# The 64-row group of the layer-3 experts' second product as two 128x64 column tiles

## The reference, cut to what matters

```python
S, E, K, C = 1024, 8, 2, 320
probs = softmax(xr @ Wg)
gate_vals, expert_idx = top_k(probs, K)
# pos: place of each (token, choice) in its expert's queue; kept = pos < C
dispatched = xr[token_of_slot].reshape(E, C, 256)
h = relu(einsum('ecd,edf->ecf', dispatched, w1))     # w1: 8 x 256 x 1024
expert_out = einsum('ecf,efd->ecd', h, w2)           # w2: 8 x 1024 x 256
out = sum over k of combine_weight[k] * expert_out[slot of (token, k)]
x = x + tanh(g_ffn[3]) * out
```

## Time and profile before

| | |
|---|---|
| median of three runs | 944.33 us (943.89 to 945.1) |
| profiled execution, span from first to last instruction | 941.6 us (the page gives no other time for it) |
| mean granted TensorE clock over the span | 0.876 of full speed |
| TensorE matmul busy | 735.4 us, 78% of the span |
| VectorE busy | 551.5 us, 59% |
| ScalarE, GpSimd busy | 372.5 us, 343.9 us |
| layer-3 experts, from the first product to the end | about 762 to 941.6 us of the span |

### The profile page before, as it was taken

How to read it: one execution, slowest core, us unless ns; L and a number is a source line. 1 busy time by engine, 2 the same in 40 slices (tenths; PEclk the granted TensorE clock), 3 DMA queues, 4 the chain that set the end, 5 groups by cost and what they waited for, 6 DMA issues and landing times.

```text
span 941.6 us, 14328 instructions
## 1 busy us (share of the span) xinstructions
PE 735.4 (78%) x5159; PEld 509.5 (54%) x5204; DVE 551.5 (59%) x1280; ACT 372.5 (40%) x673; POOL 343.9 (37%) x364
## 2 busy tenths in 40 slices
PE   5987899992567777777797992693876489999998
PEld 3444554561535555555665881362444457777776
DVE  2897847329779999989368453928676520000004
ACT  4002033222389898989520333241663122111220
POOL 2931310654137776767303715500230170000124
PEclk9997899996779898988699996696988579999999
DMA  6311217895029999999811668100013144333413
GB/s 223 127 56 46 49 42 226 195 125 48 1 44 181 170 179 163 179 164 179 174 45 45 152 122 279 42 2 0 1 42 139 46 118 142 104 103 104 149 45 117
DMA packets 139218, 102.78 MB, mean 109 GB/s; under 512 B 109714, under 2 KB 124300, under 8 KB 137102
## 3 DMA queue, kind: packets, MB, share of 16 engines
q1 hardware_dynamic: 130472, 79.10, 34.8%
q0 software_dynamic: 7760, 22.16, 11.7%
q10 hardware_dynamic: 918, 0.62, 0.2%
HBM read 65.34 MB, written 11.33 MB: 81 GB/s over the span
## 4 chain that ended last, share of the span: by engine, by line
PE 33%; issue 13%; DVE 11%; ACT 4%; DMA 3%; POOL 3%; POOLq 0%; DVEq 0%; ACTq 0%
PE psum L2291 8%; PE psum L2273 7%; PE psum L1608 3%; DVE xnT L1399 2%; PE psum L214 2%; PE psum L1885 2%; ACT both L1292 2%; DMA both<-grouped_y_dram,idx 1%; POOL both L561 1%; PE psum L1623 1%; PE psum L1208 1%; PE psum L1468 1%; DMA both<-both 1%; PE psum L614 1%; PE psum L628 1%
## 5 line engine op out<-in xcount | busy, mean ns | idle before, releaser
L1399 DVE TENSOR_SCALAR_CACHE_REDUCE xnT<-psum,both 128x1024 bf16<-128x1024 f32 x128 | 157.7, 1280 | 16.4 <-PE psum L1208 16.2
L1119 POOL TENSOR_SCALAR both<-both 128x1024 f16<-128x1024 f32 x128 | 133.7, 1045 | 83.7 <-ACT both L1292 76.8
L1292 ACT ACTIVATE both<-psum,both 128x1024 f32<-128x1024 f32 x128 | 153.7, 1208 | 14.8 <-DVE xnT L1399 14.4
L1208 PE MATMUL psum<-both 128*128 128x512 bf16 x215 | 77.5, 432 | 40.2 <-ACT both L1292 32.9
L2358 DVE COPY both<-psum 128x256 f32<-128x256 f32 (+1 forms) x21 | 8.9, 422 | 141.5 <-PE psum L2291 141.5
L2291 PE MATMUL psum<-both 128*128 128x256 f32 (+1 forms) x384 | 85.5, 380 | 0.6 <-issue 0.6
L1229 PEld LDWEIGHTS psum<-both 128*128 128x128 f16 x1024 | 64.1, 99 | 26.5 <-issue 12.7
L2273 PE MATMUL psum<-both 128*128 128x320 f32 x256 | 74.4, 445 | 3.8 <-ACT both L549 3.8
L2291 PEld LDWEIGHTS psum<-both 128*128 128x128 f32 (+1 forms) x384 | 65.4, 172 | 19.8 <-issue 3.7
L2327 ACT ACTIVATE both<-psum 128x320 f32<-128x320 f32 x64 | 28.0, 437 | 121.3 <-PE psum L2273 121.3
L1229 PE MATMUL psum<-both 128*128 128x16 f16 x1024 | 68.4, 172 | 9.2 <-DVE xn L1408 6.9
(11 more groups left out here) (373 smaller groups left out, 1525.2 us busy)
## 6 DMA issues: line engine op xcount, KB each, us to landing
both<-in_l_experts SPq DMA_DIRECT2D x50, 384.0 KB, 4.0
both<-in_l_experts SPq DMA_DIRECT2D x16, 1024.0 KB, 5.7
grouped_y_dram<-both SPq DMA_DIRECT2D x31, 128.0 KB
ctok<-in_ctx SPq DMA_DIRECT2D x2, 1024.0 KB, 8.1
both<-kpad_dram SPq DMA_DIRECT2D x1, 2048.0 KB, 8.0
moe_xn_dram<-xn POOLq DMA_DIRECT2D x4, 512.0 KB, 3.9
moe_y_dram<-both POOLq DMA_DIRECT2D x7, 256.0 KB, 4.9
both<-both SPq DMA_TRANSPOSE x96, 3.5
```

The costliest lines, as they stand in the source:

```text
L1119: nc.gpsimd.tensor_scalar(r2[n % RSLOTS2], e2[:, n % ESLOTS2, :], 255.0, HALF_BASE, ALU.mult, ALU.add).then_inc(sem("r2_ready"), 1)
L1208: last = nc.tensor.matmul(bank[2 * (n % SRING2) + half], qz2[:, h % 2, h // 2, t * P:(t + 1) * P], kT2[:, h // 2, half * 512:(half + 1) * ...
L1292: nc.scalar.activation(e2[:, n % ESLOTS2, :], scores_at(n), ACT.Exp, bias=bias2[:, n:n + 1], scale=s2[:, t * H2 + h:t * H2 + h + 1], accum ...
L1399: nc.vector.tensor_scalar(scaled2[n % 2], scores_at(n), ns2[:, t * H2 + h:t * H2 + h + 1], None, ALU.mult, ALU.min, accum_out=bias2[:, n:n ...
```

## The change

For `j == 2` each of the 8 calls of `down` becomes two: output columns 0 to 127 go to partitions 0 to 63 of bank 6, output columns 128 to 255 to partitions 64 to 127 of the same bank, both in columns 0 to 127 of it, with the same 128x64 weights loaded once for each. The copy out of PSUM is then 128 partitions by 128 columns, in place of 64 by 256, and the store of this group becomes two transfers of 64 rows and 128 columns each, so the counts on `y7_stored` rise from 32 to 48 for each expert. For expert 7 the two halves are copied by ScalarE into a zeroed `y7_last` on a diagonal: rows 0 to 63 hold columns 0 to 127, rows 64 to 127 hold columns 128 to 255, the rest is zero. The constants give partitions 64 to 127 the same slot codes as partitions 0 to 63, so that the placing product picks both halves.

```diff
--- before.py
+++ after.py
@@ -2224,7 +2224,10 @@
         moe7.diag = r.f32(NT, P)
         moe7.last_code = r.f32(NT)
         moe7.last_weight = r.f32(NT)
+        HP, HD = P // 2, D // 2
+        y7_last = r.f32(D)
         own7_code = sb("own7_code", [P, 3])
+        own7_tail = sb("own7_tail", [P, 1])
         TURN7_AFTER = (4, FC7 - 1)
 
         def l3f_sync(sp):
@@ -2288,15 +2291,22 @@
                 if e:
                     pe.wait_ge(sem("y7_ready"), 3 * (e - 1) + j + 1)
                 for f in range(FC7):
-                    last = nc.tensor.matmul(bank[4 + j][0:n, 0:D], h7[:, i, f, lo:lo + n],
-                                            w7[:, i, DC * FF7 + f * D:DC * FF7 + (f + 1) * D], start=(f == 0), stop=(f == FC7 - 1))
+                    at = DC * FF7 + f * D
+                    if j < 2:
+                        last = nc.tensor.matmul(bank[4 + j][:, 0:D], h7[:, i, f, lo:lo + n], w7[:, i, at:at + D],
+                                                start=(f == 0), stop=(f == FC7 - 1))
+                        continue
+
+                    for half in range(2):
+                        last = nc.tensor.matmul(bank[4 + j][half * HP:(half + 1) * HP, 0:HD], h7[:, i, f, lo:lo + n],
+                                                w7[:, i, at + half * HD:at + (half + 1) * HD], start=(f == 0), stop=(f == FC7 - 1))
                 last.then_inc(sem("down7_done"), 1)
 
             def own_rows(j):
-                pe.wait_ge(sem("own_y"), OWN0 + j + 1)
+                pe.wait_ge(sem("own_y"), OWN0 + (j + 1 if j < 2 else 4))
                 for t in range(NT):
                     last = nc.tensor.matmul(bank[t // 2][:, t % 2 * D:(t % 2 + 1) * D], own7[:, j, t * P:(t + 1) * P],
-                                            y7[:, LAST7 % 2, j, :], start=(j == 0 and t % 2 == 0), stop=(j == 2), skip_group_check=True)
+                                            y7[:, LAST7 % 2, j, :] if j < 2 else y7_last, start=(j == 0 and t % 2 == 0), stop=(j == 2), skip_group_check=True)
                     if j == 2 and t % 2:
                         last.then_inc(sem("own_done"), 1)
 
@@ -2327,10 +2337,14 @@
                     nc.scalar.activation(h7[:, e % 2, f, :], bank[f % 4][:, 0:C7], ACT.Relu).then_inc(sem("h7_ready"), 1)
                     if e + 1 < len(moe7.groups) and f in TURN7_AFTER:
                         moe7.turn_rows_scalar(act, e + 1, TURN7_AFTER.index(f), bank[7])
-            act.wait_ge(sem("y7_stored1"), 32 * (E7 // 2 - 1))
-            for j, (lo, n) in enumerate(JT7):
+            act.wait_ge(sem("y7_stored1"), 48 * (E7 // 2 - 1))
+            for j in range(2):
                 act.wait_ge(sem("down7_done"), 3 * LAST7 + j + 1)
-                nc.scalar.copy(y7[0:n, LAST7 % 2, j, :], bank[4 + j][0:n, 0:D]).then_inc(sem("own_y"), 1)
+                nc.scalar.copy(y7[:, LAST7 % 2, j, :], bank[4 + j][:, 0:D]).then_inc(sem("own_y"), 1)
+            act.wait_ge(sem("down7_done"), 3 * LAST7 + 3)
+            act.wait_ge(sem("own_ready"), OWN0 + 1)
+            nc.scalar.copy(y7_last[0:HP, 0:HD], bank[6][0:HP, 0:HD]).then_inc(sem("own_y"), 1)
+            nc.scalar.copy(y7_last[HP:P, HD:D], bank[6][HP:P, 0:HD]).then_inc(sem("own_y"), 1)
 
         def l3f_vector(dve, seq):
             ln_vector(dve, seq, 7)
@@ -2342,8 +2356,8 @@
             seq.step(nc.vector.tensor_tensor(moe7.weight, moe7.sel, probs7, ALU.mult))
             moe7.slots_vector(dve, seq, bank[5])
             moe7.weights_vector(seq)
-            moe7.wait(dve, "consts", 3)
-            nc.vector.memset(y7[P // 2:P, :, 2, :], 0.0).then_inc(sem("own_ready"), 1)
+            moe7.wait(dve, "consts", 5)
+            nc.vector.memset(y7_last, 0.0).then_inc(sem("own_ready"), 1)
             for half in range(2):
                 dve.wait_ge(sem("codes7_done"), half + 1)
                 for j in range(3):
@@ -2351,11 +2365,12 @@
                                             ALU.is_equal).then_inc(sem("own_ready"), 1)
             for e in range(LAST7):
                 i = e % 2
-                for j, (lo, n) in enumerate(JT7):
+                for j in range(3):
                     dve.wait_ge(sem("down7_done"), 3 * e + j + 1)
                     if e >= 2 and j == 0:
-                        dve.wait_ge(sem(f"y7_stored{i}"), 32 * (e // 2))
-                    nc.vector.tensor_copy(y7[0:n, i, j, :], bank[4 + j][0:n, 0:D]).then_inc(sem("y7_ready"), 1)
+                        dve.wait_ge(sem(f"y7_stored{i}"), 48 * (e // 2))
+                    width = D if j < 2 else HD
+                    nc.vector.tensor_copy(y7[:, i, j, 0:width], bank[4 + j][:, 0:width]).then_inc(sem("y7_ready"), 1)
 
             moe7.combine_vector(dve)
             for b in range(4):
@@ -2368,6 +2383,11 @@
             moe7.constants(pool)
             nc.gpsimd.iota(own7_code[:], pattern=[[-P, 3]], base=int(Moe.BIG) - LAST7 * C7, channel_multiplier=-1,
                            allow_small_or_imprecise_dtypes=True).then_inc(moe7.sem("consts"), 1)
+            nc.gpsimd.iota(own7_tail[:], pattern=[[0, 1]], base=int(Moe.BIG) - LAST7 * C7 - 2 * P + HP, channel_multiplier=-1,
+                           allow_small_or_imprecise_dtypes=True).then_inc(moe7.sem("consts"), 1)
+            moe7.wait(pool, "consts", 4)
+            nc.gpsimd.tensor_copy(own7_code[HP:P, 2:3], own7_tail[HP:P, :]).then_inc(moe7.sem("consts"), 1)
+            moe7.wait(pool, "consts", 5)
 
         def l3f_gpsimd2(pool):
             moe7.store_xn_gpsimd(pool)
@@ -2377,10 +2397,11 @@
                 pool.wait_ge(sem("y7_ready"), 3 * e + 3)
                 pool.dma_start(moe7.y_dram[e * C7:e * C7 + 2 * P, :].rearrange("(j p) d -> p j d", p=P), y7[:, i, 0:2, :])\
                     .then_inc(sem(f"y7_stored{i}"), 16)
-                pool.dma_start(moe7.y_dram[e * C7 + 2 * P:(e + 1) * C7, :], y7[0:C7 - 2 * P, i, 2, :])\
-                    .then_inc(sem(f"y7_stored{i}"), 16)
-            pool.wait_ge(sem("y7_stored0"), 32 * (E7 // 2))
-            pool.wait_ge(sem("y7_stored1"), 32 * (E7 // 2 - 1))
+                for half in range(2):
+                    pool.dma_start(moe7.y_dram[e * C7 + 2 * P:(e + 1) * C7, half * HD:(half + 1) * HD],
+                                   y7[half * HP:(half + 1) * HP, i, 2, 0:HD]).then_inc(sem(f"y7_stored{i}"), 16)
+            pool.wait_ge(sem("y7_stored0"), 48 * (E7 // 2))
+            pool.wait_ge(sem("y7_stored1"), 48 * (E7 // 2 - 1))
             moe7.gather_gpsimd(pool)
 
 
```

## The result

The changed kernel took 931.68 us (median of four runs, 929.94 to 934.41) beside 944.72 us for the kernel before; the ratio is 0.9863, interval 0.9839 to 0.9887. It is the rival "full overlap" (932.9 us) that came true, and not the half overlap that I had taken as the likeliest case.

A forecast was written before the change was run, and what follows sets the result against it. TensorE was taken to bound the expert stage for experts 0 to 6; -5.8 us there and +0.4 in the tail gave -5.4, so 944.33 us became 938.9. The range over the cases was 932 to 947 us, leaving out stalls.

The forecast's parts named there:

- full overlap: 64-row group: passes of both column tiles run side by side, 1.69 us saved per expert, 932.9 us; chance 0.27.
- half overlap: 64-row group: the tiles overlap by half a pass at each step, 0.83 us saved per expert, 938.9 us; chance 0.31.
- What bounds the kernel: Expert stage: TensorE on the path, so time saved in second products of experts 0 to 6 moves the end seven times.
- If B's first load also waits until A-low has started: 64-row group: upper tile's load waits for the lower tile's second pass to start; 0.328 us per chunk, 0.103 saved.
- B-high: 64-row group: first of the upper column tile's two float32 passes in a chunk, forecast to start at 0.164 us.
- chunk f: One hidden chunk of the 64-row group, eight per expert: 0.431 us before, four passes and four loads after.
- The bound of the loads: 64-row group: four 64-column loads of 0.055 us occupy the load path 0.220 us per chunk, just filling 0.218 of streaming.
- The passes and the entry: 64-row group: 0.109 us per pass of 128 columns; step to 64 columns costs 0.09 plus 0.05 us, unchanged.
- The third store: Tail after expert 6: one more POOL issue puts the last landing at +0.55 us; less 0.14 for the copy, 0.4 net.
- Expert 7 at nothing: End of the kernel: a faster 64-row group of expert 7 saves nothing, since the gathers hold the end.
- stalls rival: 64-row group: each step between tiles stalls 0.05 or 0.14 us, kernel slower at 951.2 or 962.7 us; chance 0.20.
- From span to median: Whole kernel: median of the runs taken as constantly 2.7 us above the profiled span.

The follow-up runs named there:

- same_tile: Changed kernel's 16 short calls per expert, but both halves on partitions 0 to 63, one column tile; copies and stores as before the change: 943.1 us, ratio 0.9984.
- last_expert_as_before: Changed kernel with the 64-row group of expert 7 alone in the old form, 8 calls of 256 columns and one copy: 934.74 us, ratio 0.9876.
- halves_in_turn: Changed kernel with the 8 calls of the lower tile first, then the 8 of the upper one: 940.97 us, ratio 0.9958.
- blocks_of_four: Changed kernel with four calls of the lower tile, four of the upper, four and four: 936.83 us in a single run.
- blocks_of_two: Changed kernel with two calls of the lower tile, two of the upper, and so on: 931.65 us in a single run.

## Why the prediction was wrong

- **What bounds the kernel: right.** TensorE holds the stage for experts 0 to 6, each saved 1.69 us came out at the end seven times, and no feeder was late. In front of the second products of experts 0 to 3 the path leaves TensorE for 1.2 us of ScalarE, before and after alike.
- **The step that failed: "If B's first load also waits until A-low has started."** The changed kernel's load rows show loads of both tiles side by side (4 loads in 0.20 us, where one tile alone has 2 in 0.19), and matmuls in pairs 7 ns apart from the first on. So B-high starts with A-high, ahead of A-low, a chunk f takes 0.218 us and not 0.328, and an expert saves 1.69 us and not 0.83. The row that I leaned on, a load behind each started matmul, was read in one tile alone. It still holds there (the third pair of loads starts at 787.168 us, 2 ns behind the second pair of matmuls), but it could not tell "loads wait for the matmul ahead" from "loads wait for a free place in their own tile". I took the first since a row seemed to carry it, and named the second a rival at 0.27. The runs show that a load does not wait for a matmul of the other tile; what it waits for in its own tile they leave open.
- **The bound of the loads: right for one tile, wrong in kind.** 4 x 0.055 us for each f assumed one load path. Within a tile the loads are 0.055 us apart at the closest, but those of the other tile start 7 ns beside them; that the sum of 0.220 just equalled 0.218 hid this.
- **The passes and the entry: right.** 0.109 us for 128 columns, 0.30 us and 0.05 us at the entry, 3.65 us without overlap (`same_tile`).
- **The third store: 0.55 us forecast, 0.17 measured.** The copy is 0.29 us, 0.13 less (0.14 forecast). From the copy's start to the last landing it is 3.65 us (904.00 - 900.35) against 3.61 before (910.68 + 2.17 - 909.24), so the store added 0.17. I let the landing move by the whole length of an issue. The third issue did start 0.53 us behind the second (902.20 - 901.67), but it landed 1.80 us after its start, where the last store of before took 2.17. Whether that is because it has half the bytes was not tested. Net 0.04 in place of 0.4.
- **Expert 7 at nothing: right** (`last_expert_as_before`).
- **The form change as price of the stalls rival: right as a row, wrong as a mechanism.** Going from one tile to the other of the same form costs 7 ns, not 0.14 us. Only the change between 128 and 64 columns stalls. Two of this rival's sums are also slightly off: 16 x 0.05 + 0.04 is 0.84 us and 8 x 2.28 is 18.2, which makes its prices 951.1 and 962.6 us.
- **From span to median: wrong.** I took the 2.7 us from the span to the median as constant. Here the span is 932.7 and the median 931.68, 1.0 us below it, because the profiled execution was the slowest of the four (934.41 us). That, and the slower start of the stage in this profile, are why the spans are 8.9 us apart and the medians 13.0.
- **The range** ended 0.9 us below the price of full overlap. The scatter of the runs (1.7 us below and 2.7 above the median here) was left out, and the median fell 0.3 us outside.

In the Trainium skill two rules stood against each other. The rule of the Trainium skill's page "TensorE: Matmul & The Clock Gate", Part 3, The mechanism, that loads overlap running matmuls only where row groups differ, does not hold here: both tiles have all 128 rows, and their loads and matmuls run side by side. The span model of the same page of the Trainium skill, Part 3, Measured speedup vs the span model, gives some 4 ns from tile to tile; the 7 ns here are near it. The Trainium skill's section The mechanism also has matmuls start in program order. As long as the calls alternate this trace has nothing against it call by call, but `halves_in_turn`, `blocks_of_four` and `blocks_of_two` only fit if one waiting call is passed.

## What to carry to other kernels

Here a stationary operand of 64 columns cost as much as one of 128; splitting the moving operand in two column tiles halved such a group, provided that calls of the two tiles alternate, or come in runs of at most two. Read a queueing rule only from rows in which the resource in question is free; where the rows show one tile alone, they can't tell the two readings apart. When two small stores are put into one, look at how many of its packets run side by side before counting the saved issue.

## What the hardware showed beside it

- Weight loads of two column tiles run side by side: 4 loads in 0.20 us at the start of a group, where 2 of one tile take 0.19.
- As far as four orders show, one waiting float32 call can be passed by a call of the other tile, a second not: groups of 1.92, 1.96, 2.51 and 3.27 us for runs of 1, 2, 4 and 8 calls of one tile.
- A pair of changes between the 128- and the 64-column form costs 0.35 us of TensorE, 0.15 going in and 0.20 coming out.
- Two tiles with 256 or 320 moving columns each stream at the rate of one full-width matmul (6.91 us for 64 matmuls of 256 in tiles and for 32 in full width; the first product of 320 columns takes 8.61 us tiled and 8.81 in full width, where a change of form goes ahead of it).
- One strided store of 64 KB landed after 3.68 us, its 16 packets of 4 KB two at a time, where two of 32 KB let the gathers begin 1.4 us earlier.
